# Bias attention: loops written out, the head change reordered, the shift in three parts

## What is computed

```python
q, k, v = jnp.split(qkv, [qk_dims, 2 * qk_dims], axis=-1)
...
pos = relative_position_bias(pos_q, pos_emb_h, pos_emb_w).reshape(B, nh, L, L)
scores = jnp.einsum('bnqd,bnkd->bnqk', q, k) * scale + pos
attn = jax.nn.softmax(scores, axis=-1)
out = jnp.einsum('bnqk,bnkd->bnqd', attn, v)
```

## Time and profile before

| what | value |
| --- | --- |
| runs | 9179.64, 9185.72, 9197.97 us, median 9185.72 us |
| the profiled execution | 9173.38 us, span 9171.1 us |
| TensorE matmul busy over the span | 8249.2 us (90%) |
| VectorE / ScalarE / GpSimd busy | 77% / 63% / 73% |
| mean granted TensorE clock | 0.939 |

### The profile page before, as it was taken

The page is one execution under the profiler, slowest core; times in us unless marked ns, Lnnn a source line. Parts: engine busy times, 40 slices in busy tenths (PEclk is TensorE's granted clock), DMA queues, the critical chain, the costliest instruction groups (busy, mean ns, idle before and its releaser), DMA issues. The chain is left out here.

```text
span 9171.1 us, 139845 instructions
## 1 busy us (share of the span) xinstructions
PE 8249.2 (90%) x42040; PEld 6698.1 (73%) x42040; DVE 7023.1 (77%) x7887; ACT 5757.1 (63%) x14820; POOL 6732.2 (73%) x3596
## 2 busy tenths in 40 slices
PE   6999999999999867899999999968999989888798
PEld 4766767677676633788888888855786868888775
DVE  6776767767677666899999999976777836999734
ACT  4877878778787734777777777731565623445304
POOL 3876868678696725899999999950686825999605
PEclk9999999999999977899999999988999989989898
DMA  2111111111111145544444444454000010000000
GB/s 93 28 40 30 41 40 30 41 28 44 26 42 33 56 170 202 149 104 108 107 105 110 104 107 108 106 184 151 29 23 18 23 53 19 1 1 1 20 8 19
DMA packets 480129, 596.14 MB, mean 65 GB/s; under 512 B 273736, under 2 KB 294480, under 8 KB 471568
## 3 DMA queue, kind: packets, MB, share of 16 engines
q1 hardware_dynamic: 479504, 588.17, 22.5%
HBM read 349.14 MB, written 157.03 MB: 55 GB/s over the span
## 5 line engine op out<-in xcount | busy, mean ns | idle before, releaser
L817 POOL TENSOR_TENSOR l_probs_low<-l_probs,l_probs_high 128x512 fp32r<-128x512 f32 x1792 | 2385.8, 1361 | 786.7 <-ACT l_probs_high L787 771.1
L1542 POOL TENSOR_TENSOR m_c_h<-m_h,m_c 128x2048 f32<-128x2048 f32 x520 | 2341.6, 4577 | 46.2 <-DVE m_h L1529 46.0
L1529 DVE TENSOR_TENSOR_SCAN m_h<-m_decay,m_ps_x 128x1024 f32<-128x1024 f32 x1040 | 2271.0, 2262 | 93.3 <-issue 69.3
L1442 PE MATMUL m_ps_y<-m_c_h,m_ident 128*128 128x256 f32 x8320 | 1977.9, 381 | 2.1 <-POOL m_c_h L1542 2.1
L873 DVE TENSOR_REDUCE l_max_by_row<-l_ps_all 128x8 f32<-128x512 f32 x2048 | 1357.9, 685 | 525.2 <-PE l_ps_all L636 446.3
L1442 PEld LDWEIGHTS m_ps_y<-m_c_h,m_ident 128*128 128x128 f32 x8320 | 1510.6, 190 | 173.1 <-POOL m_c_h L1542 3.7
L785 ACT ACTIVATE l_probs<-l_ps_all 128x512 f32<-128x512 f32 x2048 | 1240.5, 606 | 453.8 <-PE l_ps_all L677 310.1
L787 ACT ACTIVATE l_probs_high<-l_ps_all 128x512 fp32r<-128x512 f32 x2048 | 1233.0, 602 | 0.0
L2556 POOL TENSOR_TENSOR s_late<-s_late,s_products 128x1024 f32<-128x1024 f32 x352 | 858.3, 2481 | 314.6 <-ACT s_products L2538 314.5
L2096 POOL TENSOR_TENSOR l_probs_low<-l_probs,l_probs_high 128x512 fp32r<-128x512 f32 x512 | 664.8, 1305 | 566.0 <-ACT l_probs_high L2079 551.7
L1466 ACT ACTIVATE m_b_diagonals<-m_steps,m_b_rows 128x32 fp32r<-128x32 f32 x4160 | 966.8, 306 | 3.1 <-DMA m_b_rows<-b_t 3.1
(11 more groups left out here) (382 smaller groups left out, 13834.3 us busy)
## 6 DMA issues: line engine op xcount, KB each, us to landing
m_delta_u<-du_t SPq DMA_DIRECT2D x1040, 128.0 KB, 3.8
m_c<-c_windows SPq DMA_DIRECT2D x130, 512.0 KB, 4.3
l_q_and_row_bias<-l_q_parts SPq DMA_DIRECT2D x64, 512.0 KB, 5.1
du_t<-m_delta_u_high SPq DMA_DIRECT2D x128, 256.0 KB, 3.0
du_t<-m_delta_u_low SPq DMA_DIRECT2D x128, 256.0 KB, 2.9
ys<-m_y SPq DMA_DIRECT2D x256, 126.0 KB, 5.0
m_direction<-ys SPq DMA_DIRECT2D x12, 2048.0 KB, 14.4
l_xn<-xn SPq DMA_DIRECT2D x8, 2048.0 KB, 7.9
```

The lines of the kernel that those rows point to most:

```text
L817: pool.tensor_tensor(pl[:, slot, :], pt[:, slot, :], f(ph[:, slot, :]), ALU.subtract).then_inc(low_pool, 1)
L1442: ins = pe.matmul(y_ps[:, group % 2, 0:DIRS * SPAN].rearrange("p (d t) -> p d t", d=DIRS), ident[:, :], ch[:, group % CH, :, n, :], start= ...
L1529: dve.tensor_tensor_scan(h[:, u % H, :], decay[:, pair % 2, ct, k % 2, :, :].rearrange("p n t -> p (n t)"), x_ps[:, u % X, :], 0.0, ALU.mu ...
L1542: pool.tensor_tensor(ch[:, group % CH, 2 * pair % DIRS:2 * pair % DIRS + 2, :, :].rearrange("p d n t -> p d (n t)"), h[:, 2 * pair % H:2 * ...
```

## The change

The plan gets another order. The q jobs move from tiles 0 to 4 of block 7 to tiles 23 to 30 of block 6 (their plan tile is negative), one per tile. The h jobs come at tiles 1 to 4 of block 7, the w jobs one per tile at 5 to 12, and k6 moves from tile 26 to tile 6; to allow that, the last 1024 keys instead of 512 are kept aside for block 7 (`ASIDE`). The first units are issued one at a time, before the scores, after them and after the weighing, at tiles 15 to 26. `turn_bias` of the new block comes at tile 26, its `turn` at tile 28, so before the last tiles, and 12 of the 16 matmuls of v's second half go among the last three weighings. Six units of block 1 are made before block 0 begins (`FILL`), and 26 are left for block 0.

In every block, `turn` comes one tile later (tile 20, not 19), and the shift is three steps for VectorE at 20.3, 20.9 and 21.9, with units between. The high rows are copied as soon as they are made (semaphore `high_made`), the low rows after; for block 0 the low rows' four DMAs are issued by ScalarE's queue. `turn_bias` now uses 128 rows (64 of them zeros, cleared once by GpSimd) and `turn` 128 columns. The loop over heads on TensorE, that over blocks on ScalarE and GpSimd are written out; ScalarE and GpSimd keep a loop over heads.

```diff
@@ -406,23 +406,25 @@
-    EARLY, READY = 12, 19
-    LAST = slice(L - TW, L)
-    plan = [(0, "q", 0), (0, "q", 1), (1, "q", 2), (2, "q", 3), (2, "q", 4), (3, "q", 5), (4, "q", 6), (4, "q", 7),
...
+    EARLY, READY, FILL = 12, 19, 6
+    ASIDE = 2 * TW
+    LAST = slice(L - ASIDE, L)
+    TURN_FIRST, FILL_FIRST = 28, 2
+
+    plan = [(t - 9, "q", t) for t in range(NTB)]
+    plan += [(1, "h", 0), (1, "h", 1), (2, "h", 2), (2, "h", 3), (3, "h", 4), (3, "h", 5), (4, "h", 6), (4, "h", 7), (5, "w", 0), (5, "k", 7),
+             (6, "w", 1), (6, "k", 6), (7, "w", 2), (7, "k", 0), (8, "w", 3), (9, "w", 4), (9, "k", 1), (10, "w", 5), (11, "w", 6), (12, "w", 7),
+             (13, "k", 2), (16, "k", 3), (18, "k", 4), (22, "k", 5), (27, "v", 0), (KT, "v", 1)]
...
-    FIRST_KEYS = (7, 0, 1, 2, 3, 4, 5, 6)
-    FIRST_UNITS = {16: 3, 17: 3, 18: 3, 19: 3, 20: 3, 21: 3, 22: 2, 23: 2, 24: 2, 25: 2, 26: 2, 27: 2, 28: 2}
+    FIRST_KEYS = (7, 6, 0, 1, 2, 3, 4, 5)
+    FIRST_UNITS = {15: 2, 16: 2, 17: 3, 18: 3, 19: 3, 20: 3, 21: 3, 22: 3, 23: 3, 24: 3, 25: 2, 26: 2}
@@ -432,7 +434,7 @@
-            done, to_do = (EARLY, UNITS - EARLY) if row_in_head else (0, UNITS)
+            done, to_do = (EARLY, UNITS - EARLY) if row_in_head else (FILL, UNITS - FILL)
...
             def copy_q(it):
+                if it:
+                    sp.wait_ge(scored, scored_at(it * NTB - 2, KT - 1))
+                    sp.wait_ge(last_in, it * 48)
...
             def copy_rows(it, j):
-                sp.wait_ge(shifted, row + 2)
-                for g in range(GROUPS):
-                    for first, part in ((D, rh), (D + NEAR, rl)):
+                for first, part in ((D, rh), (D + NEAR, rl)):
+                    if part is rh:
+                        sp.wait_ge(high_made, row + 1)
+                    elif j:
+                        sp.wait_ge(shifted, row + 2)
+                    else:
+                        break
+                    for g in range(GROUPS):
                         sp.dma_start(f(ql[first:first + NEAR, slot, g, :]), f(part[g * NEAR:(g + 1) * NEAR, :])).then_inc(ql_in[slot], 16)
...
@@ -650,18 +666,19 @@
                 pe.wait_ge(shifted, row + 1)
                 for k in range(QT):
                     at = slice(j * TW + k * P, j * TW + (k + 1) * P)
-                    ins = pe.matmul(ps[:, TURNED, k * SIDE:(k + 1) * SIDE], r32[:, at], ident[0:SIDE, 0:SIDE], start=True, stop=True)
+                    ins = pe.matmul(ps[:, TURNED, k * SIDE:(k + 1) * SIDE], bias_rows[:, at], ident[:, 0:SIDE], start=True, stop=True)
                 ins.then_inc(bias_turned, 1)
             def turn(row):
                 pe.wait_ge(max_ok, row + 1)
                 for k in range(QT):
-                    ins = pe.matmul(ps[0:SIDE, TURNED, k * P:(k + 1) * P], mx[:, k:k + 1].to_broadcast((P, SIDE)), ident[:, :], start=True, stop=True)
+                    ins = pe.matmul(ps[:, TURNED, k * P:(k + 1) * P], mx[:, k:k + 1].to_broadcast((P, P)), ident[:, :], start=True, stop=True)
                 ins.then_inc(turned, 1)
...
                 if 20 <= i < 28:
                     for t in range(2):
                         project_v(it, off, 2 * (i - 20) + t)
+                if i == 26:
+                    made(it, off, number["k", 5] + 1)
+                    turn_bias(it * NTB + off * NTB, 0)
+                if i == 27:
+                    for u in range(FILL_FIRST):
+                        max_unit(it * NTB + off * NTB + 1, 1, u)
+                if i == TURN_FIRST:
+                    turn(it * NTB + off * NTB)
+
+            def first_units(it, off, i, part):
+
                 first = sum(count for tile, count in FIRST_UNITS.items() if tile < i)
-                for u in range(first, first + FIRST_UNITS.get(i, 0)):
-                    first_unit(it, off, u)
-                if i == 28:
-                    made(it, off, number["v", 0] + 1)
-                    turn_bias(it * NTB + off * NTB, 0)
+                if part < FIRST_UNITS.get(i, 0):
+                    first_unit(it, off, first + part)
 
             def attend(it, j, following):
                 row = it * NTB + j
                 for i in range(KT):
+                    if following == 2:
+                        first_units(it, 1, i, 0)
                     for block_of, u in units(j, i):
                         max_unit(it * NTB + block_of, block_of, u)
                     if j + 1 < NTB:
                         if i == 4:
                             turn_bias(row + 1, j + 1)
-                        if i == READY:
+                        if i == READY + 1:
                             turn(row + 1)
                     if i + 2 < KT:
                         score(it, j, i + 2)
                     elif j + 1 < NTB:
                         score(it, j + 1, i + 2 - KT)
-                    if following:
+                    if following == 1:
+                        begin(it, 1, i - KT)
+                    if following == 2:
+                        first_units(it, 1, i, 1)
                         begin(it, 1, i)
                     if i >= LAG:
                         weigh(it, j, i - LAG)
                     elif j:
                         weigh(it, j - 1, KT + i - LAG)
+                    if following == 2:
+                        first_units(it, 1, i, 2)
                 if j == NTB - 1:
-                    for i in range(KT - LAG, KT):
-                        weigh(it, j, i)
-                    if following:
+                    for i in range(LAG):
+                        if following == 2:
+                            for t in range(4):
+                                project_v(it, 1, KT // 2 + 4 * i + t)
+                        weigh(it, j, KT - LAG + i)
+                    if following == 2:
                         start(it, 1)
 
             def start(it, off):
                 row = it * NTB + off * NTB
-                turn(row)
-                for t in range(KT // 2, KT):
+                for t in range(KT // 2 + 4 * LAG if off else KT // 2, KT):
                     project_v(it, off, t)
-                made(it, off, number["k", 6] + 1)
-                if off:
-                    for i in range(2):
-                        score(it + 1, 0, i)
-                else:
-                    for i in range(2):
-                        score(it, 0, i)
-
-            for i in range(KT):
+                for u in range(FILL_FIRST, FILL):
+                    max_unit(row + 1, 1, u)
+                for i in range(2):
+                    score(it + off, 0, i)
+
+            for i in range(-KT, KT):
                 begin(0, 0, i)
+                for part in range(3):
+                    first_units(0, 0, i, part)
             start(0, 0)
-            with pe.Fori(0, ITS - 1) as it:
+            for it in range(ITS):
                 for j in range(NTB):
-                    attend(it, j, j == NTB - 1)
-            for j in range(NTB):
-                attend(ITS - 1, j, False)
+                    attend(it, j, max(0, j + 3 - NTB) if it + 1 < ITS else 0)
...
-            for n in range(JOBS):
+            def copy_low_rows(it, off):
+
+                act.wait_ge(shifted, it * NTB + (off * NTB + 2))
+                for g in range(GROUPS):
+                    act.dma_start(f(ql[D + NEAR:SIDE, 0, g, :]), f(rl[g * NEAR:(g + 1) * NEAR, :])).then_inc(ql_in[0], 16)
...
+            copy_low_rows(0, 0)
...
             with act.Fori(0, ITS - 1) as it:
-                with act.Fori(0, NTB - 1) as j:
+                for j in range(NTB - 2):
                     block_of(it * NTB + j)
+                for i in range(KT):
+                    exponentials(it * NTB + (NTB - 2), i)
+                    for n, (tile, kind, t) in enumerate(plan):
+                        if tile == i - 1 - KT:
+                            take(it, 1, n)
                 for i in range(KT):
                     exponentials(it * NTB + (NTB - 1), i)
                     for n, (tile, kind, t) in enumerate(plan):
                         if tile == i - 1:
                             take(it, 1, n)
+                copy_low_rows(it, 1)
                 take(it, 1, number["v", 1])
-            with act.Fori((ITS - 1) * NTB, ITS * NTB) as row:
-                block_of(row)
+            for j in range(NTB):
+                block_of((ITS - 1) * NTB + j)
...
@@ -883,9 +933,14 @@
                 dve.wait_ge(turned, row + 1)
                 chain.link(dve.tensor_tensor(r1[:, :], r32[:, j * TW:(j + 1) * TW], ps[0:SIDE, TURNED, :], ALU.subtract))
+
+            def shift_high(row):
                 if row:
                     dve.wait_ge(ql_in[(row - 1) % 2], ((row - 1) // 2 + 1) * QL_LOADS + 1)
-                chain.link(dve.tensor_copy(rh[:, :], r1[:, :]))
+                dve.tensor_copy(rh[:, :], r1[:, :]).then_inc(high_made, 1)
+
+            def shift_low(row):
+                dve.wait_ge(high_made, row + 1)
```

(12 more changed lines are left out.)

61 lines of the change are left out of this document (36 added, 25 removed).

## The result

The changed kernel took 9063.8 us (median of 4 runs, 9058.9 to 9082.4), the kernel before on the same chip 9182.7 (9177.1 to 9198.0). The ratio is 0.9872, with a 95% interval of 0.9853 to 0.9890: 119 us faster, where 227 were forecast. The time lies outside the predicted range (8885 to 9025). The profiled execution took 9058.9 us.

What follows compares the result with a forecast made beforehand. TensorE (PE), busy 90% of the span, was taken as the bound. Savings of 48 us (regular blocks), 172 (head changes), 5 and 2 sum to 227, giving 8958 us; the 8-in-10 range was 8885 to 9025.

Steps and rivals of the forecast that it cites:

- Regular blocks: Blocks 0 to 6 of each head: 1.2 us saved per block, 48 us for blocks 1 to 5 of 8 heads.
- the shift in three parts: Regular blocks: a unit's reduction can pass between the shift's steps; PE lost 0.1 us at most, counted as nothing.
- the 0.90 us of the later turn: Regular blocks: one tile later the maxima are ready when PE arrives; 0.90 us saved, at worst half.
- The wide turns: Regular blocks: 128 x 128 turns stream like the rest; 0.1 us at each of three ends, 0.30 per block.
- rival D: No change: waits only move, as when GpSimd bounds regular blocks at 41.2 us; 9170 to 9200; chance 0.02.
- In regular blocks PE does not wait for them, so nothing: Writing out ScalarE's loop over blocks and GpSimd's saves nothing in regular blocks.
- Block 6: Takes in eight q jobs, 7.0 us, less 1.2 and 0.8 of slack: 39.3 us becomes 44.3.
- Block 7: Head change: three parts of 30.5, 28.4 and 10.7 us, say 69.5, against 90.5 before.
- The third part: End of block 7, from the turn: 10.7 us against 15.9; the 5.1 us wait for low rows goes.
- Rival B: Head change: ScalarE's w copies or late low-row DMAs hold PE back; 9007 us, 8990 to 9040; chance 0.18.
- Block 0: Next head's first block: 51.5 us less 4.0 branch wait, 1.4 units, 1.2 and 2.6 clock, to 42.3.
- rival E: Slower: written-out code of PE, ScalarE and GpSimd is fetched too slowly, 4.0 us a stop; chance 0.04.

Runs made afterwards that it cites:

- low_later: Changed kernel with the low half of the shift one tile later (READY + 3.9): 9014.1 us, regular blocks 40.19 us.
- low_later_still: q_three_banks with the low half at READY + 4.9 and, in block 7, the inverse and last division earlier: 8970.3 us, regular blocks 39.21.
- before_turn_later: Kernel before with the maxima's turn one tile later and the undivided shift behind it: 9179.4 us, blocks 41.21.
- turn_back: Changed kernel with the maxima's turn and all three parts of the shift one tile earlier: 9029.1 us, blocks 40.72.
- changed_act_straight: Changed kernel with only ScalarE's loop over heads written out: 9028.1 us.
- narrow_turns: low_later with the two turns as before the change, of 64 rows and 64 columns: 9052.7 us, blocks 40.87.
- w_earlier: Kernel of low_later_still with 13 units made ahead for 12, and w jobs 4 to 7 one tile earlier: 8940.3 us.
- h_on_vector: low_later with the copies of the h jobs on VectorE instead of ScalarE: 9022.1 us.
- half_reductions: low_later with block 0's maxima reduced over half of the keys only: 8977.3 us, block 7 73.4 us.
- low_rows_on_sync: low_later with SyncE, not ScalarE, issuing block 0's four low-row copies: 9004.7 us, block 7 76.5 us.
- q_three_banks: low_later with q jobs over banks 3, 4, 7, those in 3 and 4 not waiting for the shift's low half: 9001.2 us.

## Why the prediction was wrong, by its own steps

**Regular blocks, the step that failed.** "PE lost 0.1 us there at most, counted as nothing": the price of the shift in three parts was read from where it stood before, though the change put its last part against `take_low(21)`. There the low half took 1.28 us for the 0.68 of the kernel before, beside a subtraction of GpSimd's, and PE waited 1.4 us in nearly every block. Against the best place tried, the place of the low half costs 41.35 - 39.21 = 2.14 us a block (`low_later`, 1.16 of it; `low_later_still`, 0.98 more).

"Since nothing else on VectorE moves ahead of them" was true of the maxima and said nothing of the units behind the shift, which moves with the turn. So the 0.90 us of the later turn was not there to be had by itself: with the shift undivided it came to nothing (`before_turn_later`, 41.21 for 41.18). It is worth 1.02 with the low half at READY + 3.9 and 0.53 against `turn_back`; such terms can't be added up without their places. The wide turns gave 0.68 (0.30 forecast): the places were right, the ends of the eight, but of the four only the gap ahead of the bias's turn and the late scores were counted, and not what is lost behind the first and behind the last of the eight. 41.18 - 1.02 - 0.68 = 39.48, near the 39.21 that a good placing gives; the rest was not taken apart. That GpSimd paces these blocks (rival D) is refuted by blocks of 38.94.

"In regular blocks PE does not wait for them, so nothing" failed too: the loop that stays on ScalarE costs 0.3 us in each of these blocks (41.35 to 41.04 in `changed_act_straight`).

The Trainium skill (TensorEngine Tiling (Array Packing), Key Properties) says that changing the tiling mode drains TensorE. The trace agrees for the turns, 0.34 us a turn in `narrow_turns` beside `low_later`, all of it at the ends. It does not for the h jobs, 64 columns wide too: in the changed kernel the first of a job still starts 0.23 us behind the matmul ahead of it, which is the pace, and the next matmul 0.06 us behind the last, as the job's own follow each other. So why the turns lose is not shown.

**The head change.** Block 6: 43.8 for 44.3, by terms that cancel. Head 7's block 6, without q jobs, fell by 0.4 us (39.12 to 38.69) and not by 1.2, and the q jobs cost at most 43.77 - 38.69 = 5.1 where 7.0 - 0.8 = 6.2 was forecast. Block 7: my terms were 30.5, 28.4 and 10.7; to the first unit, to the turn of the bias, and from the turn to the next head's block, they measured 32.6, 29.2 and 10.9. Between the last two, from the turn of the bias to the turn of the maxima, lie 3.75 us that stand in no term. The third part was named as 498.79 to 514.73, which holds the 5.50 us between the turns, but its sum began only at the turn: an error of adding up, 26 us over seven changes. Of the 2.1 us in the first, most is a wait of 1.4 that I had written off: that for the last w split moved to the first unit (`w_earlier` removed it, and took 1.5 us off block 7). Rival B had named ScalarE for such a case; `h_on_vector` shows that the h copies on it are not the cause, its w copies were not tested apart. In the second term VectorE is the bound (`half_reductions`), and sizing it at 28.4 for 29.2 was near. The wait for low rows went, but by the work ahead of it and not by the second queue, which `low_rows_on_sync` does without.

**Block 0.** 43.2 for 42.3, in part by luck. PE's branch was priced well: 4.0 us forecast, 4.7 measured with what follows. The branch that stays was passed over, though it had been noted: ScalarE's costs 3.0 us at each head's start (43.6 to 40.6 in the changed kernel, the registers' 0.3 in it). Without it the block takes 1.7 us less than forecast, so the other terms took off too little, and the two errors cancel in large part.

By the Trainium skill (Runtime: NRT & Kernel Launch, Instruction fetch mechanics) a branch out of the fetched window stalls. The trace agrees for PE's (the 4.0 us behind it) and for ScalarE's: in the changed kernel ScalarE's next instruction starts some 3.5 us behind the branch over heads, and in the kernel before, of its 64 branches, only six have such a stop, one at each head, of 2.4 to 2.7 us; the others have none over 0.3. GpSimd's next instruction, too, starts 2.5 to 2.8 us behind its branch in the changed kernel, but no run shows a cost for PE.

**The opening**, 4.6 us longer for 2 less. Two banks for q cost 1.9 us of its first part (`q_three_banks`). The rest is not settled: the way from the first q job to the first score varies from 78 to 83 us between kernels that do the same there (79.1 in the changed kernel, 82.9 in `low_later`, 78.3 in `turn_back`). The granted clock from 75 to 115 us varies with it: 0.83 and 0.68 in the two halves in the changed kernel, 0.76 and 0.59 in `low_later`, 0.84 and 0.74 in `turn_back`.

**Straight code** (rival E) showed no stops: no issue row of weight in any block.

## What to carry to other kernels

When an instruction is moved in an engine's order, list what stands before and behind it at the new place, with durations, up to the next one that another engine waits for; a step that cost nothing at the old place has no price yet at the new one, and its own length can change with what another engine does beside it. Where a wait is removed, the next wait at the same place is found by asking how long the engine's longest run without serving the bound engine is, against the buffers that bridge it (here 2.9 us against two banks). Sum a stretch from its first row to its last, and check that the parts add up to its length before any is changed.

## What the runs showed that I had not expected

The same VectorE instruction has more than one length: the low half of the shift took 1.28 us in the changed kernel and 0.67 in `low_later_still`, `take_low` 1.77 and 1.29, at places two reductions apart. Its shortest, median and longest time (ns) in the kernel before, in the changed one and in `turn_back`:

```profile
L889 DVE TENSOR_TENSOR l_row_bias_low<-l_row_bias_shifted,l_row_bias_high x64: 682/684/684, 125.8 to 3122.8; 64x512 fp32r<-64x512 f32 x64
L944 DVE TENSOR_TENSOR l_row_bias_low<-l_row_bias_shifted,l_row_bias_high x64: 682/1286/1674, 129.6 to 3006.5; 64x512 fp32r<-64x512 f32 x64
L944 DVE TENSOR_TENSOR l_row_bias_low<-l_row_bias_shifted,l_row_bias_high x64: 670/673/685, 128.5 to 2976.1; 64x512 fp32r<-64x512 f32 x64
```

The records of GpSimd beside it settle which overlap makes the difference. In the first and the third kernel none of the 64 starts while GpSimd subtracts. In the changed kernel 56 do, and each of them ends 0.54 to 0.55 us behind the end of that subtraction of GpSimd's, whenever it started itself; the other 8 take 0.68. `take_low` behaves alike (0.55 us behind), and GpSimd's subtraction is held in turn where VectorE's got there first: it then ends some 1.15 us behind it, in place of taking 1.29. Reductions don't show this: the 89 between 300 and 420 us of the changed kernel all take 0.67 to 0.69 us. By these numbers two subtractions that meet, one on each engine, don't run side by side, and a good place for one is where none of the other engine's runs.

And register arithmetic ahead of an engine's instructions can reach another engine: with constants on ScalarE, PE's blocks are 0.27 us shorter, in three places where the score behind a unit had been 0.09 late.
